# A gather engine's bookkeeping adds without their drains, and a static schedule placed anew with other durations

## The reference

```python
x = x + _L0_gnn_ref(adj, _layernorm(x), W, b)             # max over up to 25 neighbours, then relu([X, agg] @ W + b)
x = x + _L0_ffn_ref(_layernorm(x), Wg, ..., W2, b2)       # 8 experts, top 2, hidden 512, gelu
x = x + _L1_gnn_ref(_layernorm(x), adj, Wq, Wk, Wv, Wo)   # 8-head attention masked by adj
x = x + _L1_ffn_ref(_layernorm(x), router..., expert...)  # 6 experts, top 2, three layers of 128
```

## Time and profile before

| | |
|---|---|
| median of 3 runs | 3346.68 us (3340.56 to 3350.5) |
| the profiled execution's own time | 3350.98 us |
| its span | 3349.0 us |
| PE, DVE, ACT, POOL busy | 2576.5, 1841.5, 1339.9, 858.9 us |
| PE clock, mean over the span | 0.9 of full speed |

### The profile page before, as it was taken

How to read it: one execution, slowest core, us unless ns; L and a number is a source line. 1 busy time by engine, 2 the same in 40 slices (tenths; PEclk the granted TensorE clock), 3 DMA queues, 4 the chain that set the end, 5 groups by cost and what they waited for, 6 DMA issues and landing times.

```text
span 3349.0 us, 48458 instructions
## 1 busy us (share of the span) xinstructions
PE 2576.5 (77%) x16137; PEld 1540.5 (46%) x16137; DVE 1841.5 (55%) x5404; ACT 1339.9 (40%) x1993; POOL 858.9 (26%) x917
## 2 busy tenths in 40 slices
PE   0018628868779986898689886898779999997697
PEld 0015514524346644564356543564346655744253
DVE  5235356576358744775368633776358628526803
ACT  1004213316533654336433553236533563363163
POOL 3535515503540065103530055103540000000000
PEclk9999859869989988999889988899889999998698
DMA  5523526412621154113621165112721120012000
GB/s 136 67 40 54 67 57 105 66 45 65 102 40 39 59 83 69 29 52 65 96 37 39 61 94 58 32 46 63 102 40 38 33 45 32 20 31 47 32 1 7
DMA packets 107566, 183.70 MB, mean 55 GB/s; under 512 B 21471, under 2 KB 57724, under 8 KB 107260
## 3 DMA queue, kind: packets, MB, share of 16 engines
q0 software_dynamic: 25344, 51.96, 16.2%
q1 hardware_dynamic: 81916, 128.08, 14.4%
HBM read 158.59 MB, written 20.97 MB: 54 GB/s over the span
## 4 chain that ended last, share of the span: by engine, by line
PE 34%; DVE 30%; issue 25%; DVEq 6%; ACT 3%; DMA 2%; POOL 1%; SPq 0%; ACTq 0%; POOLq 0%
DVE tmp L1112 9%; PE PY L1387 7%; PE PH L1376 5%; PE PA L1422 4%; PE PA L1425 3%; PE PA L1399 3%; DVE G L890 3%; PE PY L1437 3%; DVE res_n L1014 2%; DVE score L858 2%; DVEq L810 2%; DVE top L862 2%; PE PH L1481 2%; PE PY L1496 2%; PE PH L1488 2%
## 5 line engine op out<-in xcount | busy, mean ns | idle before, releaser
L782 POOL DMA_INDIRECT G<-table,slot_idx x792 | 833.4, 1052 | 364.0 <-issue 364.0
L1112 DVE CUSTOM_DVE_ANT_0 tmp<-PA,mask 128x1024 bf16<-128x1024 f32 x512 | 626.9, 1224 | 41.7 <-issue 41.6
L1246 ACT ACTIVATE HB<-PA 128x1024 f32<-128x1024 f32 x512 | 498.2, 1022 | 345.2 <-PE PA L1425 343.6
L1239 ACT ACTIVATE HB<-PH,bias_T 128x512 f32<-128x512 f32 x512 | 351.6, 687 | 679.4 <-PE PH L1376 679.2
L1387 PEld LDWEIGHTS PY<-W_sb,HB 128*128 128x128 f32 x4096 | 523.1, 199 | 105.2 <-issue 71.6
L1387 PE MATMUL PY<-W_sb,HB 128*128 128x128 f32 x4096 | 529.4, 283 | 34.5 <-DVE res_n L1014 34.5
L1376 PE MATMUL PH<-XT,W_sb 128*128 128x512 f32 x1024 | 528.1, 629 | 24.9 <-ACT HB L1239 11.7
L1422 PE MATMUL PA<-QS,KS 99*128 99x512 bf16 x1024 | 408.2, 399 | 19.6 <-ACT HB L1246 15.4
L665 DVE MEMSET dve_pad<- 1x1 f32 x669 | 39.5, 59 | 689.7 <-DMA G<-table,slot_idx 550.3
L1425 PE MATMUL PA<-identb,mask 128*128 128x128 bf16 x4096 | 410.6, 224 | 0.0
L1399 PE MATMUL PA<-KS,QS 96*128 96x512 bf16 x1024 | 343.3, 421 | 74.7 <-DVE MX L1112 67.8
(11 more groups left out here) (163 smaller groups left out, 2453.4 us busy)
## 6 DMA issues: line engine op xcount, KB each, us to landing
adj_sb<-in_adj SPq DMA_DIRECT2D x64, 512.0 KB
adjm<-in_adj SPq DMA_DIRECT2D x64, 512.0 KB, 3.3
G<-table,slot_idx POOLq DMA_INDIRECT x792
parts_dram<-parts SPq DMA_DIRECT2D x16, 768.0 KB, 3.5
QS<-parts_dram SPq DMA_DIRECT2D x96, 128.0 KB, 5.8
KS<-parts_dram SPq DMA_DIRECT2D x96, 128.0 KB, 8.6
xn<-in_x SPq DMA_DIRECT2D x8, 512.0 KB, 5.1
table<-xn SPq DMA_DIRECT2D x8, 512.0 KB, 4.4
```

The source lines that it names most:

```text
L782: pool.indirect_dma_start(G[:, t % 2, s, :], None, table, bass.IndirectOffsetOnAxis(slot_idx[:, t, s:s + 1], axis=0), bounds_check=ROWS - ...
L1112: ins = dve.tensor_tensor_reduce(out=junk, in0=psum(ps, step)[:, :], in1=mask[:, t, :], scale=1.0, scalar=LOWEST, op0=ALU.add, op1=ALU.max ...
L1239: act.activation(HB[:, i % 2, c, :], psum(ps, step)[:, :], ACT.Gelu, bias=bias_T[:, e * HC + c:e * HC + c + 1]).then_inc(*emptied(ps, step))
L1246: act.activation(HB[:, kc % 2, 2 * pr:2 * pr + 2, :], psum(ps, key)[:, :].rearrange("p (h q) -> p h q", h=2), ACT.Exp, scale=float(D) ** - ...
```

## The change

Three things are changed.

1. POOL's adds: the one for `find t` writes column t of a wider `pool_pad`, the one for `pmax t-2` column 8 + t, both read two columns that nobody writes, and no drain stands behind them. One drain stands at the head of each pass's gathers.
2. PE: where a step waits for two taken banks of PSUM and both are the same bank, it waits once, for the later of the two.
3. The planner's durations: `find`, `gather` and `pmax` get other numbers, and a step gated by a gather may start only 3.0 after the gather's end (`LANDING`). This changes the order of the steps in the three filling passes and in the loop's; the three emptying passes keep theirs.

```diff
+LANDING = 3.0
@@ def course(step):
     if k == "find":
-        return [("DVE", 9.0 if step[1] == 0 else 4.5)]
+        return [("DVE", 11.2 if step[1] == 0 else 6.0 if step[1] < 3 else 3.3)]
     if k == "gather":
-        return [("POOL", 36.0 if step[1] == 0 else 23.0 if step[1] < 3 else 12.5)]
+        return [("POOL", 37.0 if step[1] == 0 else 24.0 if step[1] < 3 else 12.0)]
     if k == "pmax":
-        return [("DVE", 8.0 if step[1] == 0 else 4.0)]
+        return [("DVE", 5.0 if step[1] == 0 else 3.5 if step[1] < 3 else 2.2)]
@@ def tried(step):
-        now = max([ended[g] for g in p.gates.get(step, [])], default=0.0)
+        now = max([ended[g] + (LANDING if g[0] == "gather" else 0.0) for g in p.gates.get(step, [])], default=0.0)
@@
-        pool_pad = sb("pool_pad", [1, 4])
+        pool_pad = sb("pool_pad", [1, 2 * TILES + 2])
@@
-            if pool:
-                eng.tensor_tensor(pad[0:1, 0:1], pad[0:1, 1:2], pad[0:1, 2:3], ALU.add)
-                eng.drain()
-            else:
-                eng.memset(pad[0:1, 0:1], 0.0)
+            eng.memset(pad[0:1, 0:1], 0.0)
+
+        def pool_held_by(pool, n):
+
+            pool.tensor_tensor(pool_pad[0:1, n:n + 1], pool_pad[0:1, 2 * TILES:2 * TILES + 1],
+                               pool_pad[0:1, 2 * TILES + 1:2 * TILES + 2], ALU.add)
@@ gpsimd, def body(ps, turn, b):
                 if ps.load:
+                    pool.drain()
                     pool.wait_ge(*at(ps, turn, "tab", ("store_x",)))
                     for t in range(TILES):
                         pool.wait_ge(*at(ps, turn, "idx", ("find", t)))
-                        held_by(pool, pool_pad, True)
+                        pool_held_by(pool, t)
                         if t >= 2:
                             pool.wait_ge(*at(ps, turn, "aggr", ("pmax", t - 2)))
-                            held_by(pool, pool_pad, True)
+                            pool_held_by(pool, TILES + t)
@@ tensor (the same at gnn, lg0, down0, av, projt and lg1):
-                        for pr in range(2):
-                            pe.wait_ge(*is_taken(ps, turn, ("st", qh, g, kc, pr)))
+                        wait_taken(pe, ps, turn, ("st", qh, g, kc, 0), ("st", qh, g, kc, 1))
```

More of the change, by code:

```diff
@@ L630, in is_taken, with wait_taken @@
             return free[name], v
+        def wait_taken(eng, ps, turn, *keys):
+            last = {}
+            for key in keys:
+                name = ps.bank[key]
+                if name not in last or ps.place["bank", key] > ps.place["bank", last[name]]:
+                    last[name] = key
+            for key in last.values():
+                eng.wait_ge(*is_taken(ps, turn, key))
         def is_full(ps, turn, key):
@@ L656, in settled, with held_by @@
             return name, value if isinstance(value, int) else eng.snap(value)
-        def held_by(eng, pad, pool=False):
-            if pool:
-                eng.tensor_tensor(pad[0:1, 0:1], pad[0:1, 1:2], pad[0:1, 2:3], ALU.add)
-                eng.drain()
-            else:
-                eng.memset(pad[0:1, 0:1], 0.0)
+        def held_by(eng, pad):
+            eng.memset(pad[0:1, 0:1], 0.0)
+        def pool_held_by(pool, n):
+            pool.tensor_tensor(pool_pad[0:1, n:n + 1], pool_pad[0:1, 2 * TILES:2 * TILES + 1],
+                               pool_pad[0:1, 2 * TILES + 1:2 * TILES + 2], ALU.add)
         loads = [
@@ L1312, in body @@
                         for hf in range(2):
-                            pe.wait_ge(*is_taken(ps, turn, ("xn", hf)))
-                            pe.wait_ge(*is_taken(ps, turn, ("agg", hf)))
+                            wait_taken(pe, ps, turn, ("xn", hf), ("agg", hf))
                             key = ("gnn", hf)
@@ L1346, in body @@
                     elif kind == "lg0":
-                        pe.wait_ge(*is_taken(ps, turn, ("t0", 0)))
-                        pe.wait_ge(*is_taken(ps, turn, ("t0", 1)))
+                        wait_taken(pe, ps, turn, ("t0", 0), ("t0", 1))
                         pe.wait_ge(*is_free(ps, turn, ("lg0",)))
@@ L1382, in body @@
                         if tt == 0:
-                            for c in (HC - 2, HC - 1):
-                                pe.wait_ge(*is_taken(ps, turn, ("up0", i, c)))
+                            wait_taken(pe, ps, turn, ("up0", i, HC - 2), ("up0", i, HC - 1))
                             pe.wait_ge(*is_free(ps, turn, key))
@@ L1451, in body @@
                         qh = step[1]
-                        pe.wait_ge(*is_taken(ps, turn, ("ctx", qh, 0)))
-                        pe.wait_ge(*is_taken(ps, turn, ("ctx", qh, 1)))
+                        wait_taken(pe, ps, turn, ("ctx", qh, 0), ("ctx", qh, 1))
                         transposes(ps, turn, ("ctxT", qh), ctxn, 0)
@@ L1470, in body @@
                     elif kind == "lg1":
-                        pe.wait_ge(*is_taken(ps, turn, ("r1", 0)))
-                        pe.wait_ge(*is_taken(ps, turn, ("r1", 1)))
+                        wait_taken(pe, ps, turn, ("r1", 0), ("r1", 1))
                         pe.wait_ge(*is_free(ps, turn, ("lg1",)))
```

## The result

| | before | after |
|---|---|---|
| median | 3344.73 us (4 runs) | 3046.41 us (3043.21 to 3052.26, 4 runs) |
| ratio, 95% interval | 1 | 0.91 (0.9087 to 0.9114) |
| the profiled execution, its span | 3350.98, 3349.0 us | 3052.26, 3050.2 us |

What follows compares the result with a forecast made beforehand. No engine is full; POOL's gather line, with drains between tiles, holds DVE and PE up. Savings of 182 us in the loop and 106 in the filling passes, 288, take 3350.98 to 3063, stated as 3060; range 3000 to 3160.

Steps and rivals of the forecast that it cites:

- The drains: On POOL between tiles: the 4.08 us idleness is the drain; without it the gap falls from 5.9 to 1.8 us.
- the drain does nothing: Rival: the first DMA or reading the class itself waits for landing, so the 4.08 us stay; 3347 us, chance 0.04.
- A gap of 1.8 us, "I keep all of it": On POOL between tiles: two adds of 0.18 and 1.41 us of reading the class remain without drains.
- The line: POOL's gathers in a loop pass, first add to last issue: 182 us falls to 147, saving 35 per pass.
- The landing: Rival: DMAs land at 1.74 us each, line 169 us, 3243; half-way, with collisions, 3163; chance 0.20 for the two.
- The port's collisions: POOL's DMAs stall beside DVE's two-input maxima: 1.5 us at each of 8 `pmax`, at most 12 us a line.
- The head's drain and PE's waits: One drain more per pass, hidden by POOL's idling for `find 0`; PE's merged bank waits: nothing from either.
- +3 for the moved steps, -2 for the hold: Loop pass: steps moved ahead of `pmax 7` shorten the tail by 3 us; holding `pmax 4` behind `sm` costs 2.
- the moved steps in full: Rival: 11.5 us off each loop tail and 18 off the third filling pass; 2980 us, chance 0.13.
- Filling passes: The three filling passes save 33, 35 and 38 us, together 106.
- Loop: Five loop passes save 36 us each, 180, and 2 more for the one with 105 DMAs: 182.
- slower: Rival: `pmax 4` held until `gather 6` idles; 3387 us with slow gathers, needs over 50 us hold if faster; chance 0.03.

Runs made afterwards that it cites:

- drains_only: The changed kernel with the planner's old durations and no landing time, so the order of the kernel before: 3074.88 us, ratio 0.9196.
- one_drain: The changed kernel with a drain put back behind the first of the two adds only: 3269.04 us, ratio 0.9772.
- eight_slots: The changed kernel with every tile gathering 8 slots without reading its class, 64 DMAs a pass: 2957.35 us, ratio 0.8837.
- order_only: The kernel before with the planner's new durations and LANDING; POOL's adds and drains and PE's waits stay: 3285.74 us, ratio 0.9825.

## Why the prediction was right

**The drains.** Right: the 4.08 us were the drain, behind the first add, and its removal is the gain (`drains_only`, `one_drain`). The rival "the drain does nothing" falls with it. *A gap of 1.8 us, "I keep all of it"* was too much where nothing else holds POOL: without a drain the class is read ahead, and a gap is 0.34 us with one add and about 0.5 with two. The first filling pass shows it, 40.1 us shorter where I had 33, all of it in POOL's line (177.5 to 137.4 us). Where POOL stands at a wait, reading the class costs its 1.1 us as before; `eight_slots`, which doesn't read it, has 0.52 there.

**The line.** Predicted 147 us, measured 146, for a reason partly different: gaps shorter, but 6.6 us of waiting for `pmax`, 5.21 of them ahead of tile 4. That the two nearly cancel is luck. That pass gains 36.6 us, predicted 36.

**The landing.** The rival had the DMAs land at 1.74 us each. Over the whole line they did not: POOL issues all 97 in 146 us, and the last packets land at 1172.75, 4.3 us after the last issue (1168.41), as they did behind tile 6 of the kernel before (1338.77 to 1343.28, 4.5). But in the middle of the stage the landing does set the pace. The last DMA of tile 2, then the end of DVE's wait for that tile, then the windows of that stretch and of the one behind it:

```profile
1102.82 0.99 POOL L794 DMA_INDIRECT G<-table,slot_idx  x1 [0.30 <-issue]
...
1115.50 0.06 DVE L671 MEMSET dve_pad<- 1x1 f32 x1 [8.91 <-DMA G<-table,slot_idx]
...
1100.00:1116.00 16.00, 11.78 (x50) 6.31 (x50) 5.83 (x26) 7.01 (x11) 11.72 (x14) 1.00 0.98 158
1116.00:1169.00 53.00, 42.40 (x203) 25.59 (x204) 39.43 (x133) 26.20 (x44) 34.73 (x39) 0.90 0.41 64
```

Tile 2 lands 12.7 us after its last issue, at a DMA share of 0.98, while SP's loads of the adjacency and of the stacks take 36% of the engines' time and the gathers 62%, and `pmax 2` can't start before. So the 5.21 us for which POOL waits ahead of tile 4 come from the landing and not from a busy DVE. This agrees with the page DMA: Bandwidth & Descriptors (section Issuing engines are not separate DMA queues) of the Trainium skill, that DMAs started by different engines run on the same 16 DMA engines. The stage's mean share, 0.61 where the earlier trace rows had 0.52, hides it. So the rival was right for a tile or two of a pass: in three of the loop's passes POOL waited 2 to 6 us because of it, where the rival had 23. One reading in its favour was loose: the 6.50 us behind 25 DMAs hold the 1.41 us of reading the class, which the 4.08 behind 8 do not.

The port's collisions did not cost more either. Single DMAs that meet a maximum on DVE still last longer:

```profile
1142.01 1.19 DVE L902 TENSOR_TENSOR G<-G 128x512 f32<-128x512 f32 x2 [0.67 <-issue]
...
1155.28 1.19 DVE L902 TENSOR_TENSOR G<-G 128x512 f32<-128x512 f32 x2 [0.65 <-issue]
```

Beside these stand a DMA of 1.23 us (at 1142.84) and one of 1.45 (at 1155.39), which agrees with the rule of GPSIMD Engine Reference (section Key points) of the Trainium skill. By the records of all DMAs 39 met such a maximum in the kernel before, 1.39 us long on average, and 95 do now, 1.17 us long; the others take 1.04 in both. So the collisions became more, but each is shorter, and the mean rose only from 1.052 to 1.059: 792 x 0.007 = 5.5 us over the kernel, where my estimate had up to 12 in each of eight passes.

**The head's drain and PE's waits.** Nothing, as predicted. The drain at the head has 97 DMAs behind it and ends 9 us after the last issue by its record, and POOL then idles until `find 0`, 192.62 us in all. That it lies under this cover was read, not tried by leaving it out.

**The order.** *"+3 for the moved steps, -2 for the hold"* gives 1 a pass; on fast gathers it gives 19.8 in the loop, 4.0 a pass on average, but from pass to pass -1.8, 0.5, 2.3, 7.3 and 11.5. I was right not to believe in the moved steps in full: in the third filling pass they gave 2.6 of their 18 us. My reason was wrong, though. I had PE too busy to take them; in fact they took 17.6 us off the end of the pass and put 14.9 on POOL's line, by the wait for `pmax`. They do pay in full where gathers are slow (`order_only`, 17.6 of 18 there), which the prediction did not ask.

**The sum.** Filling passes: 106 predicted, 124 measured. The term that was too small is the line's saving, by the gaps; 40.1 for 33 and 45.4 for 35, the second with a PE clock up from 0.80 to 0.87. The third, 38.4 for 38, is right by luck: I had 35 from the line and 3 from the moved steps, and it was 25.7 from the line and 12.9 from the end of the pass. Loop: 182 predicted, 172.6 measured. The shortfall stands in two passes, of 26.6 and 31.0 us. In those POOL waits for `pmax` ahead of four tiles:

```profile
775.89 0.18 POOL L675 TENSOR_TENSOR pool_pad<-pool_pad 1x1 f32<-1x1 f32 x1 [6.12 <-DVE dve_pad L919]
...
791.74 0.18 POOL L675 TENSOR_TENSOR pool_pad<-pool_pad 1x1 f32<-1x1 f32 x1 [3.73 <-DVE dve_pad L919]
...
805.96 0.18 POOL L675 TENSOR_TENSOR pool_pad<-pool_pad 1x1 f32<-1x1 f32 x1 [2.63 <-DVE dve_pad L919]
...
819.24 0.18 POOL L675 TENSOR_TENSOR pool_pad<-pool_pad 1x1 f32<-1x1 f32 x1 [0.60 <-DVE dve_pad L919]
```

13.1 us in the first of the loop's passes and 9.9 in the third, against 6.6 in the second. `drains_only` waits 9.6 and 9.7 us for `pmax` in these two passes, so most of it comes with the fast gathers and not with the order. Some of it is again the landing: ahead of the first row's 6.12 us DVE had itself waited 8.51 us for the DMAs of tile 2. For the other three tiles `pmax` came 9 to 12 us behind the landing, because DVE had other steps ahead of it: the mechanism of the rival "slower", at a few us where it needed 50. The two errors, +18 and -9, are both of the size of a gap's detail, and the forecast of 3060 for 3046 owes something to their opposite signs.

**The clock.** In the loop's pass PE's work is 309.05 x 0.96 = 297 us of full clock, as before (294), at a granted clock of 0.96 where the earlier trace rows had 0.92: 10 us less of busy time, with fewer stops ahead of it. The tail behind `pmax 7` runs at 1.00:

```profile
1022.00:1170.00 148.00, 124.45 (x850) 69.58 (x848) 81.85 (x237) 83.32 (x133) 105.88 (x111) 0.92 0.61 94
...
1184.00:1306.50 122.50, 118.92 (x653) 80.27 (x652) 94.67 (x248) 36.81 (x54) 0.00 (x0) 1.00 0.11 36
```

**What stays open.** What holds the loop's pass at 340 us, 37 above one that gathers nothing, was not taken apart: `eight_slots` leaves 332 on average with hardly a wait for gathers. The wait for a tile's class (119.5 us over the kernel) makes me suspect the single adjacency buffer, but no run gives it a second one. Nor was it tried whether the adds need columns of their own once the drains are gone.

## What to carry to other kernels

A drain on the engine that issues DMAs is a wait for those DMAs: look for idleness that nothing ends between two small instructions, and see whether the drain can go when each write gets a place of its own. The gain of taking out a stall and that of reordering around it are not added: the reordering fills the same waiting, so it is worth most where the stall stays (60 us here) and less where it goes (28), since the moved steps then hold up the engine that was freed. And ask what a freed engine will wait for next; here it was the buffer that DVE empties (56 us over the kernel), in part because DVE came late and in part because the DMAs themselves landed late. A mean hides the second: look at the DMA share tile by tile.

## What the runs showed of the hardware

- A drain on POOL waits for more than the last landing. Behind it comes a time that grows with the number of indirect DMAs issued since the drain before: 0.4 us for 1, 0.7 for 8, 1.0 for 16, 3 to 5 for 65 to 105. With nothing in flight it lasts 0.27 us for none, 0.94 us for 8 DMAs and 5.59 for 65, so an estimate from the last two is 0.08 us for each DMA, part of which goes on beside the landing. So the rarer a drain, the longer it lasts.
- POOL reads a value from SBUF into a register ahead of the DMAs that it has still to issue, if no drain or wait stands between: from the end of the add to the next tile's first DMA 0.15 us, where a wait makes it 1.1 and a drain 1.41 us.
- The landing of a tile's gather follows the DMA share: 12.7 us after the last issue at a share of 0.98, 4.3 us at the end of the line, in a stretch with a share of 0.41.
- An indirect DMA of 128 rows costs POOL 1.02 to 1.06 us and 0.30 of idleness in every kernel run here, whatever stands around it.
